# First layer's expert drain: end paddings moved to SyncE and GpSimd, expert sends moved behind them, ring depths changed

## The reference

```python
x = x + tanh(g_xattn[0]) * L0_xattn(layernorm(x), ctx, ctx, mask, ...)   # 16 heads
x = x + tanh(g_ffn[0])   * L0_ffn(layernorm(x), Wg, W1, b1, W2, b2)
x = x + tanh(g_xattn[1]) * L1_xattn(layernorm(x), ctx, ctx, ...)
x = x + tanh(g_ffn[1])   * L1_ffn(layernorm(x), ...)                     # 16 experts, top 2

def L0_ffn(x, Wg, W1, b1, W2, b2):          # 8 experts, top 1
    top1 = argmax(x @ Wg.T, axis=-1)
    for e in range(8):
        h = gelu(x @ W1[e] + b1[e], approximate=False)   # 128 -> 512
        y = h @ W2[e] + b2[e]                            # 512 -> 128
        out = where(top1 == e, y, out)
    return out
```

## Time and profile before

| | |
|---|---|
| Three runs | 513.42, 516.75, 519.32 us (median 516.75) |
| The profiled execution | 511.04 us, its span in the trace 509.1 us |
| Busy share of the span | PE 86%, DVE 69%, ACT 63%, PEld 63%, POOL 50% |
| Attention of the first layer with the drain | to about 203 us |
| Expert tiles 13 to 38 | PE's transposes at 209.44 to 256.83 us |
| Chain that ended last | PE 43%, DVE 19%, issue 15%, POOL 11%, ACT 7%, DMA 3% |

### The profile page before, as it was taken

How to read it: one execution, slowest core, us unless ns; L and a number is a source line. 1 busy time by engine, 2 the same in 40 slices (tenths; PEclk the granted TensorE clock), 3 DMA queues, 4 the chain that set the end, 5 groups by cost and what they waited for, 6 DMA issues and landing times.

```text
span 509.1 us, 21940 instructions
## 1 busy us (share of the span) xinstructions
PE 439.4 (86%) x8481; PEld 322.0 (63%) x8481; DVE 352.2 (69%) x885; ACT 320.8 (63%) x764; POOL 256.8 (50%) x333
## 2 busy tenths in 40 slices
PE   2698999999988795999997898998998697779996
PEld 1455676767655685999983565666666475445553
DVE  5767879888768765555536778788898587644554
ACT  2456566766856773777745465768777467775653
POOL 2632535647456177445557527454545326634454
PEclk9999999999989998999999899999999999999999
DMA  7125333312001143332114121201041000000112
GB/s 210 52 57 145 91 99 107 103 53 61 25 24 34 40 102 95 87 93 67 39 36 104 24 44 23 45 25 25 13 98 32 14 5 3 2 2 16 42 48 64
DMA packets 39446, 28.60 MB, mean 56 GB/s; under 512 B 12224, under 2 KB 34368, under 8 KB 39344
## 3 DMA queue, kind: packets, MB, share of 16 engines
q1 hardware_dynamic: 29104, 14.61, 11.3%
q0 software_dynamic: 3424, 6.51, 5.1%
q10 hardware_dynamic: 6816, 6.08, 4.2%
HBM read 19.42 MB, written 7.76 MB: 53 GB/s over the span
## 4 chain that ended last, share of the span: by engine, by line
PE 43%; DVE 19%; issue 15%; POOL 11%; ACT 7%; DMA 3%; SPq 0%; POOLq 0%; ACTq 0%; DVEq 0%
PE T_ps L899 8%; DVE maxes L625 7%; POOL y_mid L1173 7%; PE S_ps L888 6%; DVE prob L633 4%; PE A_ps L914 4%; PE m_H_ps L1484 3%; PE S_ps L882 2%; PE Q_ps L869 2%; PE m_X_ps L1511 2%; PE m_T_ps L1524 2%; PE Q_ps L781 2%; PE m_X_ps L1495 2%; POOL sorted_rows L490 2%; PE Q_ps L792 2%
## 5 line engine op out<-in xcount | busy, mean ns | idle before, releaser
L625 DVE TENSOR_REDUCE maxes<-S_ps 128x16 f32<-128x1024 f32 x64 | 78.2, 1221 | 49.4 <-PE S_ps L888 49.4
L441 POOL TENSOR_TENSOR k_blk<-kT,col_a 128x512 f32<-128x512 f32 x64 | 68.4, 1079 | 74.5 <-ACT kT L514 53.8
L556 ACT ACTIVATE probT<-T_ps 128x512 f32<-128x512 f32 x128 | 76.1, 594 | 45.0 <-PE T_ps L899 44.0
L899 PE MATMUL T_ps<-col_a,prob 128*128 128x128 f32 x512 | 84.1, 288 | 15.1 <-DVE prob L633 11.3
L899 PEld LDWEIGHTS T_ps<-col_a,prob 128*128 128x128 f32 x512 | 56.8, 144 | 55.1 <-issue 29.4
L633 DVE TENSOR_TENSOR prob<-S_ps,maxes 128x512 f32<-128x512 f32 x128 | 82.4, 685 | 2.2
L1173 POOL DMA_INDIRECT y_mid<-f_out,f_rows x39 | 37.2, 955 | 31.7 <-DVE f_out L1054 29.3
L914 PE MATMUL A_ps<-v_blk,probT 128*32 128x18 f32 x4096 | 49.0, 187 | 1.6 <-issue 1.6
L914 PEld LDWEIGHTS A_ps<-v_blk,probT 128*32 128x32 f32 x4096 | 42.3, 111 | 11.3 <-issue 10.5
L1043 DVE TENSOR_TENSOR f_hid<-f_H_ps,f_b 128x512 f32<-128x512 f32 x39 | 27.0, 692 | 29.5 <-PE f_H_ps L1225 24.6
L888 PE MATMUL S_ps<-k_blk,qT 32*64 32x256 f32 x1024 | 46.3, 411 | 0.8 <-ACT qT L550 0.3
(11 more groups left out here) (201 smaller groups left out, 873.5 us busy)
## 6 DMA issues: line engine op xcount, KB each, us to landing
f_w<-in_W ACTq DMA_DIRECT2D x16, 256.0 KB, 2.7
ctxT<-in_ctxT SPq DMA_DIRECT2D x12, 256.0 KB, 3.0
f_rows<-sorted_rows SPq DMA_DIRECT2D x39, 64.5 KB, 1.9
out<-m_final SPq DMA_DIRECT2D x32, 64.0 KB, 1.6
x_all<-in_x SPq DMA_DIRECT2D x6, 256.0 KB, 6.2
x_all<-y_mid POOLq DMA_DIRECT2D x6, 256.0 KB, 4.5
ctxT<-in_ctxT SPq DMA_DIRECT2D x8, 128.0 KB, 2.4
mask_in<-in_mask SPq DMA_DIRECT2D x6, 128.0 KB, 3.1
```

The source lines that it names most:

```text
L441: nc.gpsimd.tensor_tensor(k_blk[:, t % 2, :, :, :], kT[:, g.at(R), t - g.first, :].rearrange("p (b k) -> p b k", b=2).unsqueeze(2).to_broa ...
L556: nc.scalar.activation(probT[:, t % 2, 4 * h:4 * h + 4, :], T_ps[:, :, :], ACT.Exp, scale=SCALE).then_inc(probT_ready, 1)
L625: nc.vector.tensor_reduce(maxes[:, t % 2, :, :], S_all[:, :, 0:HQ * S].rearrange("p r (e k) -> p r e k", k=S), X, ALU.max).then_inc(max_re ...
L899: last = nc.tensor.transpose(T_ps[:, j, :], pair, ident[:, :])
```

## The change

- The paddings of experts 0 to 3 stay on SP's queue, those of experts 4 to 7 go to POOL's queue. ACT issues none. Each queue has its own semaphore.
- In the drain, sends that were due before 39 are due at 39. The scatters are earlier in the list of steps, so POOL's order is now: all scatters, its four paddings, sends 0 to 4 and on.
- Eight output buffers (`DEEP`) instead of four, with eight `sent` semaphores.
- Twelve row buffers (`RINGS`) instead of sixteen. The condition `t >= RINGS` in `load` thereby holds from tile 12 on, the last of the 13 tiles that SP loads in the drain.

```diff
 def experts0(nc, ctx, space, r, done):
-    RINGS = 16
-    DEEP = 4
+    RINGS = 12
+    DEEP = 8
     HIDS = 3
+    PADS_BY_SYNC = 4
...
-    ends_padded = sem("ends_padded")
+    ends_padded = {n: sem("ends_padded_" + n) for n in ("sync", "gpsimd")}
...
             if t == FULL_TILES:
                 sp.wait_ge(table, 2)
                 sp.wait_ge(r["padded"], 16)
-                sp.wait_ge(ends_padded, 16 * E0)
+                sp.wait_ge(ends_padded["sync"], 16 * PADS_BY_SYNC)
+                sp.wait_ge(ends_padded["gpsimd"], 16 * (E0 - PADS_BY_SYNC))
                 for s in done["scattered"][1]:
                     sp.wait_ge(s, 16 * (NT - FULL_FROM) // 4)
             row = sp.value_load(entry(0, t), min_val=0, max_val=ROWS - P)
             if t >= RINGS:
                 sp.wait_ge(sent[(t - RINGS) % DEEP], 16 * ((t - RINGS) // DEEP + 1))
...
     def drain_sync(sp):
-        return [(load(sp), range(FULL_TILES), lambda t: FULL_AT + 2.5), (pad_ends(sp, range(0, E0, 2)), once, lambda _: REST_AT)]
+        return [(load(sp), range(FULL_TILES), lambda t: FULL_AT + 2.5), (pad_ends(sp, range(PADS_BY_SYNC), ends_padded["sync"]), once, lambda _: REST_AT)]
...
+    def drain_gpsimd(pool):
+        (send, skew), = tile_gpsimd(pool)
+        return [(pad_ends(pool, range(PADS_BY_SYNC, E0), ends_padded["gpsimd"]), once, lambda _: REST_AT),
+                (send, range(FULL_SLOTS - skew), lambda t: max(slot_at(t + skew), REST_AT))]
...
-        return [(warm, once, lambda _: NT - 0.5)] + placed(sooner, 0.1) + [(pad_ends(eng, range(1, E0, 2)), once, lambda _: REST_AT)] + placed(later)
+        return [(warm, once, lambda _: NT - 0.5)] + placed(sooner, 0.1) + placed(later)
...
-                  "y_sent": [sem(f"f0_sent{k}") for k in range(4)],
+                  "y_sent": [sem(f"f0_sent{k}") for k in range(8)],
```

More of the change, by code:

```diff
@@ L1148, in load, with pad_ends @@
         return step
-    def pad_ends(eng, experts):
+    def pad_ends(eng, experts, padded):
         def step(_):
@@ L1155, in step @@
                 row = eng.value_load(pad_at[0:1, e:e + 1], min_val=0, max_val=E0 * REGION - P)
-                eng.dma_start(r["sorted"][bass.ds(row, P), :], r["pads"][:, e, :]).then_inc(ends_padded, 16)
+                eng.dma_start(r["sorted"][bass.ds(row, P), :], r["pads"][:, e, :]).then_inc(padded, 16)
         return step
     def drain_sync(sp):
-        return [(load(sp), range(FULL_TILES), lambda t: FULL_AT + 2.5), (pad_ends(sp, range(0, E0, 2)), once, lambda _: REST_AT)]
+        return [(load(sp), range(FULL_TILES), lambda t: FULL_AT + 2.5), (pad_ends(sp, range(PADS_BY_SYNC), ends_padded["sync"]), once, lambda _: REST_AT)]
     def sync(sp):
@@ L1259, in experts0 @@
     stage.sync, stage.gpsimd, stage.scalar, stage.vector, stage.tensor = sync, gpsimd, scalar, vector, tensor
-    return stage, {"sync": drain_sync, "gpsimd": lambda pool: placed(tile_gpsimd(pool)), "scalar": drain_scalar,
+    return stage, {"sync": drain_sync, "gpsimd": drain_gpsimd, "scalar": drain_scalar,
                    "vector": drain_vector, "tensor": drain_tensor}
```

## The result

| | before | after |
|---|---|---|
| Median of four runs each | 515.09 us | 522.87 us |
| Lowest and highest | 511.59, 519.32 | 518.64, 525.03 |
| Profiled execution, its span | 511.04, 509.1 | 522.95, 521.3 |
| Mean granted clock of PE in it | 0.982 | 0.967 |

The changed kernel is slower: 1.0179 times the time before, with a 95% interval of 1.0124 to 1.0234. The ratio is of the fast runs alone and so is not that of the medians in the table (1.015).

A forecast was written before the change was run, and what follows sets the result against it. From 203.5 us PE alone bounds the drain, so tile 13's transpose decides: +6.8 for its delay, +1.6 cold clock, +0.1 semaphores make +8.5 on 511.04, 519.5 us; scaled to the median 525, range 517 to 531.

The forecast's parts named there:

- The chain: End of first layer's drain: SP's paddings wait for load 12, that for send 0, that for POOL's paddings; tile 13 +6.8 us.
- Step 1 and 2: POOL, last rows known at 195.11 us: scatter 30 starts at 195.39, two scatters at 1.26 us each, free at 197.91.
- Step 3: POOL's four paddings ahead of send 0: 1.26 us each, 5.04 us together, to 202.95; bounds 0.95 and 2.1 each.
- Step 4 and 5: Send 0 starts at 202.95 us, lands 2.22 later; SP issues load 12 and the second-layer load, reaching its paddings at 206.1.
- Step 6 to 8: SP's four paddings end at 210.9 us, last lands at 213.6, then remaining loads; tile 13 there at 216.2, not 209.44.
- The cold stretch: PE's low clock after idling before tile 13: one round's "up" and "down" at 1.85 instead of 1.06 us each, +1.6 us.
- Eight semaphores: Second layer's start waits on eight semaphores instead of four: one more SP step, +0.1 us (nothing to 0.4).
- Costed at nothing: Drain: eight output buffers, late sends cleared by POOL, and twelve row buffers afterwards were each put at no cost.
- (a): Rival: SP's paddings are not held and go out at 195.9 us; 0 to +1.6 us, about 512 us; chance 0.10.
- (b): Rival: full gain from ACT freed at tile 8, load 12 and paddings early enough; -4.6 us, 506.4; chance 0.05.
- (c): Rival: DVE keeps POOL from making descriptors, each padding losing 2.17 us; +17 us, 528; chance 0.05.

## Why the prediction was right, step by step

The forecast was 525 us by a sum of +8.5; measured are 522.87 and, in the trace, +7.5. The 525 were scaled from a median of 516.75 us; from the 515.09 us of the four runs the same sum gives 523.7. The chain itself is what the experiments bear out: load 12 behind send 0, SP's paddings behind load 12. The steps, each as time after the last rows are known:

- **Step 1 and 2** (two scatters, POOL free at +2.80): the first scatter starts 0.28 us behind its release, as put; POOL takes the first padding at +2.50, since no gap of 0.30 stands between a scatter and it.
- **Step 3** (four paddings at 1.26 = 5.04 us): mis-sized. They take 3.95 us (202.49 to 206.44), the first two 0.82 and 1.14, one DMA being 0.54 to 0.60 of it and the wait for the register load most of the rest. The value lies almost at the lower bound (3.80), not at the nearest row. Send 0 starts at +6.45 instead of +7.84. That is most of the difference at tile 13.
- **Step 4 and 5** (landing 2.22, then two issues): send 0 to SP's first padding took 4.08 us, 3.89 predicted (202.95 to 206.1 and 0.74 more).
- **Step 6 to 8** (four paddings, their landing, the remaining loads, tile 13 on board): from SP's first padding to the next load 7.08 us, predicted 7.51; from there to PE's transpose 1.96, predicted 1.85. Tile 13 at +19.57, predicted +21.1; it moved by 5.2 us, not 6.8.
- **The cold stretch** (+1.6, bounds 0 and twice): 2.2 us. The second round was still partly cold, which the sum had not counted.
- **Eight semaphores** (+0.1): nothing seen; last send to end 245.0 against 245.2 us.
- **Costed at nothing**: eight output buffers, the late sends and twelve buffers in the steady state. PE is busy for 47.00 of 47.00 us from 226 on, and tile 16 to the last send takes 48.8 us both times (68.80 - 20.01, 76.29 - 27.49). Right. The cover of the output buffers is thin, though: with seven, PE lost 1.14 us to DVE in the thirteen-buffer kernel.

Two errors partly cancel, and that is luck: 1.5 us too much in the wait, 0.6 too little in the cold clock.

The rivals: (a), SP's paddings not held, is out: they stand at 210.52 (+10.53), not at +0.8. (b), the full gain of 4.6 us, was there at tile 9 (+4.07 against +8.75) and gone by tile 13. (c), DVE keeping POOL from its descriptors, is out for this stretch: the padding at 203.31 took 0.57 us across DVE's longest operation there, seen in DVE's timeline of after,

```profile
203.22 0.69 DVE L1044 TENSOR_TENSOR f_hid<-f_H_ps,f_b 128x512 f32<-128x512 f32 x1 [0.54 <-issue]
```

and those beside it 0.54 to 0.60. The row on which (c) was priced is also another thing than it was taken for. It was DVE that lost the 2.17 us there, and POOL was not issuing DMAs but computing for most of that time, in the kernel before:

```profile
268.08 2.73 POOL L441 TENSOR_TENSOR k_blk<-kT,col_a 128x512 f32<-128x512 f32 x2
```

The Trainium skill (SBUF — State Buffer, "SBUF: two separate sides") gives some five times the time for a GpSimd DMA that overlaps a VectorE copy, 3100 ns for 620; no run here shows that for these operations. As an estimate from these two figures, the difference of 2.48 us for each of four paddings is some 10 us, not the 20 us of the prediction.

What the prediction did not see is how small the parts are by themselves. It put the loss down to the chain and was right, but did not ask what each link costs alone; measured, late sends with twelve row buffers cost 0.9 us and the moved paddings gain 1.3, each in one execution and neither beyond what two executions of one kernel differed by.

## What to carry to other kernels

A wait for a free buffer is a wait of the whole queue it stands on: before cutting a ring, list what stands behind the first load that will have to wait, and what the send that frees it stands behind. Two moves that each cost little alone can cost much together, when a stall that one of them removes had hidden the wait that the other makes. Here one more buffer, or one load placed behind four paddings, took 8 us out again. And count from a moment ahead of the waits that the change makes: of 12.2 us between two traces, 4.9 lay before them.

## What the runs showed of the hardware

- A plain DMA of 128 rows issued by POOL kept it for 0.54 to 0.60 us, little more than half an indirect one (0.96). Where each waited for its register load the period was 0.82 to 1.14 us; where the four loads had been done ahead of them, 0.56.
- The clock fell in the drain at times after short idle times: in the second execution with paddings on three queues PE had been idle for 0.77 and 0.93 us since the last rows, and was granted 0.54 from 203 to 206 us; the first execution of the same kernel had much the same idle times and 1.00.
- The granted clock falls in the second layer at other places in each execution. In two kernels, the two executions of each differ by 2.9 and 3.8 us behind the last send. One execution had 0.50 from 427 to 445 us while PE was busy for 15.71 of these 18 us, as the table by stretches of the kernel with load 12 last shows:

```profile
427.00:445.00 18.00, 15.71 (x156) 11.39 (x149) 9.80 (x40) 11.02 (x34) 10.87 (x21) 0.50 0.01 2
```

What sets these falls stays open, and so does how much of the differences they make. The differences are as large as the gains that were left to find in the drain, so a trace of one execution does not settle such a gain; the timed ratio over many runs is what can.
